# Two float32r products for the sum over equal tokens, in four more pairs of a mixture-of-experts block

## The reference

```python
x_ec = xf[tok_ec]                                   # (64 experts, 64 slots, 512)
g = silu(einsum('ech,ehi->eci', x_ec, w_gate))      # i = 384
u = einsum('ech,ehi->eci', x_ec, w_up)
y = einsum('eci,eih->ech', g * u, w_down)
contrib = (y * w_ec[..., None]).reshape(-1, h)
combined = zeros_like(xf).at[tok_ec.reshape(-1)].add(contrib)
combined = combined + silu(xf @ w_sh_gate) * (xf @ w_sh_up) @ w_sh_down
```

## Time and profile before

| what | value |
|---|---|
| median of 3 runs | 696.03 us (695.61 to 696.84) |
| the profiled execution | 696.56 us |
| its span in the profile | 694.7 us |
| TensorE busy | 658.8 us, 95% of the span |
| VectorE busy | 316.5 us, 46% |
| ScalarE busy | 162.8 us, 23% |
| GpSimd busy | 219.8 us, 32% |
| moved by transfers | 203.95 MB, mean 294 GB/s |

### The profile page before, as it was taken

How to read it: one execution, slowest core, us unless ns; L and a number is a source line. 1 busy time by engine, 2 the same in 40 slices (tenths; PEclk the granted TensorE clock), 3 DMA queues, 4 the chain that set the end, 5 groups by cost and what they waited for, 6 DMA issues and landing times. The chain is left out here.

```text
span 694.7 us, 8795 instructions
## 1 busy us (share of the span) xinstructions
PE 658.8 (95%) x3165; PEld 389.7 (56%) x3165; DVE 316.5 (46%) x750; ACT 162.8 (23%) x268; POOL 219.8 (32%) x210
## 2 busy tenths in 40 slices
PE   4999999999999898999999999999999999999982
PEld 2687878878878753444454454445444444444430
DVE  5887567849958682222233222323323323232321
ACT  5923114633211411211111111112112111111210
POOL 5537446535558222021221220203220122212112
PEclk9999999999999999999999999999999999999997
DMA  8201005722875988999999999999999999999973
GB/s 321 81 7 55 1 31 191 266 74 79 314 265 205 347 325 326 402 405 404 391 399 400 363 399 386 403 369 388 387 405 385 370 385 388 402 396 366 394 225 44
DMA packets 53628, 203.95 MB, mean 294 GB/s; under 512 B 7878, under 2 KB 8262, under 8 KB 53201
## 3 DMA queue, kind: packets, MB, share of 16 engines
q1 hardware_dynamic: 37504, 170.06, 61.3%
q0 software_dynamic: 9072, 21.52, 13.0%
q10 hardware_dynamic: 7008, 11.80, 4.5%
HBM read 179.48 MB, written 24.13 MB: 293 GB/s over the span
## 5 line engine op out<-in xcount | busy, mean ns | idle before, releaser
L657 POOL DMA_INDIRECT out_dram<-ym,midx x32 | 51.3, 1604 | 282.2 <-DVE ym L1266 130.4
L1613 PE MATMUL bank<-w_sb,xT 128*64 128x384 f32 x768 | 129.1, 489 | 0.8 <-ACT xT L884 0.8
L1398 PE MATMUL bank<-x_hi,w_parts 128*128 128x512 f32 x368 | 115.3, 396 | 2.2 <-DVE x_lo L997 2.2
L1613 PEld LDWEIGHTS bank<-w_sb,xT 128*64 128x64 f32 x768 | 53.0, 137 | 71.0 <-issue 67.8
L1398 PEld LDWEIGHTS bank<-x_hi,w_parts 128*128 128x128 f32 x368 | 70.0, 191 | 18.0 <-DVE x_lo L997 3.0
L1398 PE MATMUL bank<-x_lo,w_parts 128*128 128x512 f32 x184 | 71.0, 395 | 0.0
L1201 DVE TENSOR_TENSOR sg<-sg,bank 128x384 f32<-128x384 f32 x32 | 17.8, 555 | 116.6 <-PE bank L1613 62.6
L1531 PE MATMUL bank<-sh_sb,xS 128*128 128x384 f32 x208 | 69.2, 486 | 0.0
L1634 PE MATMUL bank<-w_sb,guT 128*64 128x512 f32 x288 | 65.9, 592 | 2.8 <-DVE ym L1266 2.8
L1531 PEld LDWEIGHTS bank<-sh_sb,xS 128*128 128x128 f32 x208 | 38.7, 191 | 24.1
L911 ACT ACTIVATE y<-bank,wcol 128x512 fp32r<-128x512 f32 x26 | 17.9, 687 | 121.3 <-PE bank L1634 121.3
(11 more groups left out here) (189 smaller groups left out, 939.1 us busy)
## 6 DMA issues: line engine op xcount, KB each, us to landing
w_sb<-in_L_ffn_w_down SPq DMA_DIRECT2D x48, 768.0 KB, 21.1
w_sb<-in_L_ffn_w_gate SPq DMA_DIRECT2D x48, 768.0 KB, 16.6
w_sb<-in_L_ffn_w_up SPq DMA_DIRECT2D x48, 768.0 KB, 19.5
extra<-in_L_ffn_w_gate SPq DMA_DIRECT2D x16, 768.0 KB, 20.1
extra<-in_L_ffn_w_up SPq DMA_DIRECT2D x16, 768.0 KB, 19.9
extra<-in_L_ffn_w_down SPq DMA_DIRECT2D x16, 768.0 KB, 22.7
ring<-in_L_attn_x SPq DMA_DIRECT2D x14, 256.0 KB, 3.7
xS<-xt_dram SPq DMA_DIRECT2D x13, 256.0 KB, 18.2
```

Source lines behind the costliest of these rows:

```text
L657: pool.indirect_dma_start(out=out[:, :], out_offset=bass.IndirectOffsetOnAxis(ap=midx[j % 3][u][:, :], axis=0), in_=ym[u][:, :], in_offset ...
L1398: ins = pe.matmul(ps[u][:, :], w, xp, start=(n == 0), stop=(n == len(parts) - 1))
L1613: ins = pe.matmul(ps[e * C:(e + 1) * C, 0:I], xT[:, c, e * C:(e + 1) * C], gate_up(2 * j + u, e, k)[:, c, :], start=(c == 0), stop=(c == K ...
```

## The change

in_parts becomes true for every pair but the two of the last group. On VectorE, low_part is then issued in every group (for the second pair of the group before in all but the first, for the first pair of its own group in all but the last).

```diff
@@ -241,7 +241,7 @@
 
         def in_parts(j, u):
 
-            return has_shared(j + u)
+            return j < GROUPS - 1
 
         def gate_up(p, e, k):
             return matrix(p, e, k).rearrange("p (c n) -> p c n", c=KC)
@@ -1305,7 +1305,7 @@
                 columns(j, 0)
                 gated(j, 0)
                 turn_copy(j, 0)
-                if shared and not first:
+                if not first:
                     low_part(j - 1, 1)
                 columns(j, 1)
                 if first:
@@ -1318,10 +1318,9 @@
                 gated(j, 1)
                 if shared:
                     turn_copy_shared(item(j))
-                    turn_copy(j, 1)
+                turn_copy(j, 1)
+                if not last:
                     low_part(j, 0)
-                else:
-                    turn_copy(j, 1)
                 merged_out(j, 0)
                 same_tokens(j, 1)
```

## The result

The changed kernel takes 696.88 us (median of 12 runs, 696.14 to 698.19), the kernel before, run beside it, 695.63 us. The ratio is 1.0016 with a 95% interval from 1.0009 to 1.0023: 1.1 us slower (0.6 to 1.6), a loss that is clear of zero. The 1.1 us lie within 0.2% of the time, 1.4 us; the upper end of the interval lies outside. The profiled execution took 697.36 us with a span of 695.5.

What follows compares the result with a forecast made beforehand. TensorE was taken to set the pace of the groups, and GpSimd's chain of indirect adds the end. 0.74 - 0.14 + 0 = 0.60 us gave 696.6 us by the median; own range 696.0 to 696.9, whole range 694.9 to 698.5.

Steps and rivals of the forecast that it cites:

- Products: TensorE's merge in the four new pairs: two float32r products take 0.74 us where one float32 took 1.06, saving 0.32.
- The added wait: Merge in the four new pairs waits for low_part behind turn_copy, so TensorE is 0.74 us later each time.
- The early delay passes on to (12,0): Pair (0,0)'s delay finds no wait to vanish in, so pair (12,0)'s add starts 0.74 us later.
- What the stream gives back: At the weight stream's end, later adds have less stream beside them: 0.14 us given back, bounds none and all.
- The late delays add nothing: In the last group, TensorE's 2.78 us wait for ym takes the three late delays, 2.22 us: 0 added.
- the rival of four delays: In the last group all four delays reach the end: 3.0 us slower, 699.0 us; chance 0.12.
- the shorter products win: At merge, low_part is ready when the product would start; (0,0) gains 0.32 us: 695.7 us; chance 0.04.
- nothing arrives: The end of the weight stream takes back the whole 0.74 us: 696.0 us; chance 0.10.
- The adds fall otherwise against the stream: In the last chain of adds, shifted starts change add times: 694.4 us or 698.1 us; chance 0.08 each.

Runs made afterwards that it cites:

- e3: The change, but the four new pairs make no low rows and sum the high rows twice; +0.1 us (-0.6 to 0.7) against the kernel before.
- e7: The whole change, with low_part ahead of turn_copy on VectorE in groups without a shared tile; +0.9 us (0.3 to 1.5) against the kernel before.
- e1: The kernel before with only pair (0,0) of the four new pairs changed; +0.8 us (0.1 to 1.4) against the kernel before.
- e12: The whole change once more, a second profile and timing; +1.3 us (0.7 to 1.9) against the kernel before.
- e5: The kernel before with only pair (0,0) changed and its low_part computed four times more; +3.9 us (2.9 to 4.9) against the kernel before.
- e6: The kernel before with only (13,1), (14,0), (14,1) changed, low_part computed twice more in each; +4.8 us (3.8 to 5.8) against the kernel before.
- e4: The whole change, with merge in the four new pairs between the next pair's gate and up products; +0.9 us (0.3 to 1.5) against the kernel before.
- e10: The whole change, with batches of shared tiles added after groups 2, 5, 8, 11 and 13; -2.9 us (-3.9 to -2.0) against the kernel before.
- e9: The kernel before, with batches of shared tiles added after groups 2, 5, 8, 11 and 13; 692.97 us against 696.06, ratio 0.9955.

## Why the prediction was right

The forecast was 696.6 us, +0.6, against 696.03; measured were +1.1 us (0.6 to 1.6) and, again, +1.3 (0.7 to 1.9). It lies on the lower edge. The sign, the place and the size of one delay were right, but the sum explains only about half of the loss as timed: with each term as measured it is 0.67 us, and some 0.5 us more has no term in it. The two intervals just reach down to 0.67, so this rest is likely and not proven.

That the forecast time, 696.6, comes within 0.3 us of the measured 696.88 is in part luck: the forecast built on a median of three runs, 696.03, where twelve gave 695.63. The forecast's own range, up to 696.9, was too narrow: +0.8 is less than the middle of both measured changes. By its steps:

- **Products:** the 0.74 us for both float32r products with a load ahead of them is 0.67. The exposed load was priced at its whole 0.19 us, but the second load starts 0.11 us after the first, not behind it; from there to the next load it is 0.56 us, where 0.55 was reckoned. That they save was right, and e3 shows it with the sign and the size that xT leaves.
- **The added wait:** y_low is what comes last, its computation starting 0.48 us after turn_copy and taking 0.74; one delay is 0.67 us where 0.74 was forecast. e7 shows that turn_copy ahead of it is 0.26 us of that.
- **The early delay passes on to (12,0):** right, 0.66 us in three executions (after, e1, e12), and with the size of the delay in e3 (-0.19), e7 (0.40) and e5 (5.26).
- **What the stream gives back:** 0.14 us was forecast, and here the size was off. The premise that the stream doesn't move with TensorE is only partly so: in e5 it ended some 2 us later. With the delay of 5.26 us e5 shows a part given back; with 0.66 us nothing of it is seen. In both executions after, the chain is 85.3 us, in the two before 84.9 and 85.3, so what is left is no giving back and up to 0.4 us more that the scatter of the transfers covers. Counted from the anchor to the end of the span the change is 412.3 us in both executions, before 411.2 and 411.6: +0.7 to +1.1 us. With (0,0) alone it is 412.5, with the late three alone 411.8 and 411.1, so these profiles put the loss on the early delay. With 0 in place of 0.14 the sum would be 0.67.
- **The late delays add nothing:** in the profiles this is right. They were taken from TensorE's wait (2.8 us before, 0.7 to 1.2 us in the four executions that have them and nothing else altered), and the first and the last copy into ym waited for landings throughout. The cover behind the wait was 2.8 us and not 0.9, so the point at which the rival of four delays decides is about 5.6 us, 1.9 us each. e6 passed that point and TensorE set the end.
- **Open:** the timings of the late three alone, +0.6 us twice. Taken together, about 0.1 to 1.0, they make a small cost likelier than none, and with e1's 0.8 us the sum is about that of the change. The profiles have no step for it that is larger than their scatter. So where the 0.5 us above the sum arise is not shown: in the late pairs, in the transfers of the chain, or in both.

Of the rivals, "the shorter products win" falls with the wait for y_low in the profile, and "nothing arrives" with the two timings of the change, whose intervals begin at 0.6 and 0.7 us. "The adds fall otherwise against the stream" didn't decide, but its scatter is real: the step with the batch of yS took 16.52 and 16.65 us in the two executions before and 16.17 and 16.44 in the two after.

## What to carry to other kernels

In this kernel, splitting a float32 product in two float32r products saves time on the array only where something stands between the copy that makes the high rows and the product; with nothing there, the chain of copy, low rows and signal costs more than the products gain (0.67 us later, where the products alone came 0.20 us earlier). Before moving a product out of such a gap, see what it covers in turn: here merge covered the wait for xT. And a loss at the front of the long row of equal groups was carried whole to its end, while in the profiles the same loss in the last groups disappeared as long as other things ended later; count all the pieces of that cover, not the first wait alone, and look whether the chain that makes the cover (here ordered adds beside a weight stream) can itself be shortened, which was worth 3.1 us.

## What the runs showed of the hardware

- Equal idle times didn't cost the same clock. At the end of 4.2 us of idle weight loads in e5 it fell to 0.50, the 1.2 GHz level. In e6 the same 2.65 us of idle time came three times: after the first the clock stayed at 1.00, over 4 us after the second it was 0.61 in the mean, after the third 0.57 (both levels in one stretch). In the kernel before, TensorE's 2.78 us in the last group were followed by a clock of 1.00.

```profile
645.00:649.00 4.00, 2.77 (x16) 1.36 (x18) 2.82 (x9) 0.00 (x0) 1.20 (x1) 1.00 1.02 423
...
659.00:663.00 4.00, 4.00 (x17) 1.62 (x18) 1.68 (x7) 0.00 (x0) 0.00 (x0) 0.61 1.07 352
```

- Going between weight tiles of 64 and 128 columns, the weight loads stood idle for 0.60 us on the way in and 0.37 us on the way out (e4), where between steady pairs of loads of 64 columns they stand idle for 0.18 us. The type of the product changes in the same places, so e4 doesn't tell the one from the other.
- An indirect add that names VectorE's copy as what released it may not have waited for it: in e10 the add of (15,0) starts 0.12 us before the copy that it is put down to in e9 and in the kernel before.
